# A macaron block on one core: layer-norm rows turned by DMA in float16 parts instead of by TensorE in float32

## The reference

```python
def _layernorm(x, axis=-1, eps=1e-05):
    m = jnp.mean(x, axis=axis, keepdims=True)
    v = jnp.var(x, axis=axis, keepdims=True)
    return (x - m) / jnp.sqrt(v + eps)

x = L0_attn_x                                   # (1, 4096, 256) float32
x = x + 0.5 * ffn(_layernorm(x))
x = x + attn(_layernorm(x))
x = x + 0.5 * ffn(_layernorm(x))

# ffn(x): six routed experts of rank 16, the two largest gates kept, beside a shared one
base_out = x @ base_W.T + base_b
shared_out = (x @ shared_A.T) @ shared_B.T
gate = softmax(x @ router_W.T + router_b)       # top 2, divided by their sum: sparse_w
routed_out = sum_e sparse_w[e] * (x @ routed_A[e].T) @ routed_B[e].T

# attn(x): 16 heads of 16, layer norm of q and k inside each head, causal
q, k, v = x @ Wq.T, x @ Wk.T, x @ Wv.T
dot = (norm(q) * s) @ (norm(k) * s).T           # s = 256 ** -0.25
out = softmax(causal(dot)) @ v
return out @ Wo.T + bo
```

## Time and profile before

| | |
|---|---|
| median of the runs | 1194.99 us |
| the three runs | 1192.07, 1194.99, 1195.09 us |
| span of the profiled execution, first to last instruction | 1192.3 us |
| PE busy | 1104.1 us (93% of the span) |
| ACT busy | 1014.7 us (85%), of it 982.2 us in the 1056 exponentials |
| DVE busy | 467.5 us (39%) |
| POOL busy | 241.6 us (20%) |
| chain of waits | 72% PE, 13% ACT, 6% issue, 6% DVE |

### The profile page before, as it was taken

One profiled execution on the slowest core, in us unless ns is written; L12 is line 12 of the kernel. 1 busy time (PEld: TensorE's weight loads), 2 busy tenths in 40 slices (PEclk: granted clock), 3 DMA queues, 4 the chain that ended last, 5 costly groups with the idle time before them and its releaser, 6 DMA issues.

```text
span 1192.3 us, 22761 instructions
## 1 busy us (share of the span) xinstructions
PE 1104.1 (93%) x8884; PEld 359.6 (30%) x8884; DVE 467.5 (39%) x1181; ACT 1014.7 (85%) x1134; POOL 241.6 (20%) x377
## 2 busy tenths in 40 slices
PE   3758999999999999999999999999999999999994
PEld 3534333332323233232332232232222222222123
DVE  5678665554544353333333323423131222021114
ACT  3216788789888998999999999999999999999980
POOL 2236533222122211212022021012110101010100
PEclk9779999999999999999999999999999999999996
DMA  5022202003000300003000022000001100000000
GB/s 145 3 63 60 59 11 81 1 28 99 1 1 19 93 17 1 1 32 92 4 1 1 1 67 60 1 1 2 1 10 48 53 1 1 10 10 1 1 19 18
DMA packets 39608, 33.37 MB, mean 28 GB/s; under 512 B 8722, under 2 KB 39432, under 8 KB 39496
## 3 DMA queue, kind: packets, MB, share of 16 engines
q1 hardware_dynamic: 37364, 31.74, 9.0%
q10 hardware_dynamic: 2132, 0.12, 0.1%
HBM read 18.73 MB, written 12.85 MB: 26 GB/s over the span
## 4 chain that ended last, share of the span: by engine, by line
PE 72%; ACT 13%; issue 6%; DVE 6%; DMA 1%; POOL 1%; SPq 0%; ACTq 0%; DVEq 0%; POOLq 0%
PE ps L1190 68%; ACT ring L776 13%; PE ps L1232 2%; PE ps L1298 1%; DMA x<-in_x 1%; DVE st L807 1%; PE ps L1252 1%; DVE area L828 1%; DVE oT L1159 0%; POOL rstd L711 0%; POOL sq L532 0%; DVE x L980 0%; DVE ss L985 0%; DVE sq L1013 0%; ACT area L765 0%
## 5 line engine op out<-in xcount | busy, mean ns | idle before, releaser
L776 ACT ACTIVATE ring<-ps 128x1024 f32<-128x1024 f32 x1056 | 982.2, 1115 | 65.5 <-PE ps L1190 63.5
L1190 PE MATMUL ps<-ring,vf 128*17 128x512 f32 (+3 forms) x4608 | 559.4, 562 | 5.0 <-DVE oT L1159 4.4
L1190 PE MATMUL ps<-queries,keys 50*128 50x512 f16 (+3 forms) x2304 | 363.2, 366 | 22.1 <-ACT ring L776 4.9
L1190 PEld LDWEIGHTS ps<-queries,keys 50*128 50x128 f16 x2304 | 92.3, 93 | 475.3 <-ACT ring L776 437.3
L724 POOL TENSOR_SCALAR_AFFINE_SELECT ring<-ring 128x256 f32<-128x256 f32 (+1 forms) x224 | 103.9, 481 | 396.5 <-ACT ring L776 392.6
L1190 PEld LDWEIGHTS ps<-ring,vf 128*17 128x17 f32 x4608 | 79.7, 95 | 174.5 <-issue 144.2
L711 POOL TENSOR_TENSOR rstd<-var,minus_half 128x4 f32<-128x4 f32 x24 | 24.4, 1017 | 235.6 <-DVE var L813 235.4
L980 DVE SCALAR_TENSOR_TENSOR x<-ps,power,x 128x512 f32<-128x512 f32 x32 | 24.0, 750 | 110.7 <-PE ps L1190 110.7
L846 DVE CAST xnT<-ps 128x512 f16<-128x512 f32 x32 | 22.1, 691 | 100.0 <-PE ps L1232 100.0
L1190 PE MATMUL ps<-baseT,xnT 128*128 128x256 f16 x384 | 55.0, 283 | 3.9 <-DVE area L848 3.8
L1232 PE MATMUL ps<-ident,area 128*128 128x128 f32 x192 | 34.2, 311 | 20.0 <-DVE area L828 20.0
(11 more groups left out here) (153 smaller groups left out, 670.5 us busy)
## 6 DMA issues: line engine op xcount, KB each, us to landing
parts_d<-split SPq DMA_DIRECT2D x32, 256.0 KB, 2.6
keys<-parts_d SPq DMA_DIRECT2D x96, 64.0 KB, 2.3
queries<-parts_d SPq DMA_DIRECT2D x192, 32.0 KB
x<-in_x SPq DMA_DIRECT2D x8, 512.0 KB, 4.2
out_x<-x SPq DMA_DIRECT2D x16, 256.0 KB, 2.2
queries<-shift_d SPq DMA_DIRECT2D x64, 4.0 KB
ring<-in_base_W SPq DMA_DIRECT2D x1, 256.0 KB, 4.9
ring<-in_Wq SPq DMA_DIRECT2D x1, 256.0 KB, 3.8
```

The costliest lines, as they stand in the source:

```text
L776: act.activation(probs[:, u % RING, :], bank(2 * (u % SLOTS), 2), ACTF.Exp, bias=0.0, scale=1.0).then_inc(exp_ok, 1)
L1190: return pe.matmul(o, lhsT, rhs, start=start, stop=stop, skip_group_check=True)
```

## The change

Layer-normed rows are no longer turned on TensorE. `turn{ln}` (c, a) is now: DVE casts two scaled tiles to float16 (the high part) and subtracts it (the low part), by tokens, in SBUF; then SP issues one DMA that transposes these 128 partitions x 1024 float16 numbers, eight blocks of 128x128, into `xnT`. The readers wait for that DMA's semaphore (`t_in`), not for a copy out of PSUM. `scale` of both halves now writes one small buffer, `xn`, so it alternates with `turn`. `xnT` and the parts of the attention's output are laid out by tiles. To make room, small buffers move into `ring` or are shared. Matrices, weights, the other transposes (`turnin`, `heads`) and the numbers in `PRELUDE` and `PLACES` stay.

```diff
-    for a in range(2):
+        # front() and prepare(): turn (c, a) now directly behind scale (c, a)
         yield 1.5, f"turn{ln}", (c, a)
...
-SPLIT_STAGES = ("turn0", "turn1", "turn2", "turnin0", "turnin1")
+SPLIT_STAGES = ("turnin0", "turnin1")
...
+            if stage in TURNS:
+                self.matmuls[stage, n] = through.get(int(stage[-1]))
             if stage in BANK_STAGES:
                 i = len(self.use)
+                through[turned_rows(stage, n)] = i + 1
...
+            def turn(K, stage, n):                       # on SP
+                (c, a), i = n, int(stage[-1])
+                sp.wait_ge(K.xs_ok[i], 2 * c + a + 1)
+                if K.matmuls[stage, n]:
+                    sp.wait_ge(K.ready, K.matmuls[stage, n])
+                if i == 2 and c == 0 and a == 0:
+                    sp.wait_ge(K.w_ok, NW)
+                sp.dma_start_transpose(xnT[i][:, 2 * a:2 * a + 2, :, :, :].rearrange("p n s b t -> p (n s b) t"),
+                                       xs[i][:, 2 * a:2 * a + 2, :, :].rearrange("p n s d -> p (n s d)")).then_inc(K.t_in[i][a], 16)
...
+            def split_rows(K, stage, n):                 # on DVE
+                (c, a), i = n, int(stage[-1])
+                high, src = moved(stage, n, None)
+                low = moved(stage, n, None, 1)[0]
+                if c >= 1:
+                    dve.wait_ge(K.t_in[i][a], 16 * c)
+                dve.wait_ge(K.xn_ok[i], 2 * c + a + 1)
+                dve.tensor_copy(high, src).then_inc(*K.own.up())
+                dve.wait_ge(*K.own.at())
+                dve.tensor_tensor(low, src, high, ALU.subtract).then_inc(K.xs_ok[i], 1)
...
-            def turn(K, ln, c, a):                       # on PE
-                key = (f"turn{ln}", (c, a))
-                b = side_bank(K, key)
-                pe.wait_ge(const, NCONST)
-                pe.wait_ge(K.xn_ok[ln], 2 * c + a + 1)
-                for ib in range(2):
-                    for i in range(2):
-                        m = pe.transpose(b[:, ib * D + i * P:ib * D + (i + 1) * P], xn[ln][:, 2 * a + i, ib * P:(ib + 1) * P], ident[:, :])
-                m.then_inc(K.ready, 1)
...
                 for a in range(2):                       # inner; project and value likewise
-                    pe.wait_ge(*K.done[f"turn{2 * f}", (c, a)])
+                    pe.wait_ge(K.t_in[2 * f][a], 16 * (c + 1))
```

More of the change, by code:

```diff
@@ L295, in general_order, with turned_rows @@
         yield stage, n
-BANK_STAGES = ("sizes", "turn0", "turn1", "turn2", "inner0", "inner1", "turnin0", "turnin1", "outer0", "outer1", "qk", "value", "heads",
+TURNS = ("turn0", "turn1", "turn2")
+BANK_STAGES = ("sizes", "inner0", "inner1", "turnin0", "turnin1", "outer0", "outer1", "qk", "value", "heads",
                "projout")
-SPLIT_STAGES = ("turn0", "turn1", "turn2", "turnin0", "turnin1")
+SPLIT_STAGES = ("turnin0", "turnin1")
+def turned_rows(stage, n):
+    if stage in ("inner0", "outer0"):
+        return 0
+    if stage in ("qk", "value"):
+        return 1
+    if stage == "projout":
+        return 1 if n[0] == NC - 1 else 2
+    return 2 if stage in ("inner1", "outer1") else None
 def on_scalar(stage, n):
-    if stage == "turn0":
-        return n[0] <= 3
     if stage == "turnin0":
         return n <= 3
-    if stage in ("turn1", "value"):
+    if stage == "value":
         return n[0] <= 2
-    if stage == "turn2":
-        return n[0] == NC - 1
     if stage == "turnin1":
@@ L348, in __init__ @@
         self.high_act = s("high_act")
+        self.xs_ok = [s(f"xs_ok{i}") for i in range(fronts + 1)]
+        self.t_in = [[s(f"t_in{i}_{a}") for a in range(2)] for i in range(fronts + 1)]
         self.xn_ok, self.var_ok, self.rstd_ok = ([s(f"{q}{i}") for i in range(fronts + 1)] for q in ("xn_ok", "var_ok", "rstd_ok"))
@@ L354, in __init__ @@
         self.parts_out = [s(f"parts_out{b}") for b in range(4)]
-        self.k_in = [[s(f"k_in{c}_{i}") for i in range(2)] for c in range(NC)]
+        self.k_in = [[s(f"k_in{c}_{i}") for i in range(2)] for c in range(2)]
         self.q_in = [s(f"q_in{g}") for g in range(NG)]
@@ L415, in build @@
         qn = area[1][:, :].rearrange("p (n c) -> p n c", n=TC)
-        xnT = [sb(f"xnT{i}", [P, 2, 2, CH], F16) for i in range(3)]
-        turners = xnT[2][:, :, :, :].rearrange("p s a t -> p (s a t)").bitcast(F32).rearrange("p (k c) -> p k c", c=P)
+        xnT = [sb(f"xnT{i}", [P, TC, 2, 2, P], F16) for i in range(3)]
+        turners = xnT[2][:, :, :, :, :].rearrange("p n s a t -> p (n s a t)").bitcast(F32).rearrange("p (k c) -> p k c", c=P)
         ones_sq = turners[:, NW, :]
@@ L557, in moved @@
         def moved(stage, n, b, part=0):
-            if stage in ("turn0", "turn1", "turn2"):
-                c, a = n
-                i = int(stage[-1])
-                return xnT[i][:, part, :, a * D:(a + 1) * D], bank(b).rearrange("p (b t) -> p b t", b=2)
+            if stage in TURNS:
+                a, i = n[1], int(stage[-1])
+                return xs[i][:, 2 * a:2 * a + 2, part, :], xn[:, :, :]
             if stage in ("turnin0", "turnin1"):
@@ L641, in _ @@
                     sp.dma_start(xg, x_v[:, c * TC:(c + 1) * TC, :]).then_inc(gen_in, 16)
-                    for b in BLOCKS:
-                        write_parts(gen, c, b)
+                    for stage, n in general_order(c):
+                        if stage in TURNS:
+                            turn(gen, stage, n)
+                        elif stage == "heads":
+                            write_parts(gen, *n)
                     for g in range(NG):
@@ L1090, in _ @@
             dve.wait_ge(*own.at())
[L1091 removed]
+            dve.tensor_reduce(bound[:, 4:8].unsqueeze(2), gain_rows, AX.X, ALU.add).then_inc(*own.up())
             dve.reciprocal(per, near).then_inc(*own.up())
@@ L1277, in project @@
                 for i in range(2):
-                    pe.wait_ge(*K.done["turn1", (c, i)])
+                    pe.wait_ge(K.t_in[1][i], 16 * (c + 1))
                 for ib in range(2):
-                    m = mm_parts(b, lambda s: xnT[1][:, s, ib, t], lambda s: qkT[:, s, ib, :], ib == 0, ib == 1)
+                    m = mm_parts(b, lambda s: xnT[1][:, k, s, ib, :], lambda s: qkT[:, s, ib, :], ib == 0, ib == 1)
                 m.then_inc(K.ready, 1)
@@ L1305, in front_and_heads @@
                     sizes(K, n)
-                elif stage == "turn0":
-                    turn(K, 0, *n)
-                elif stage == "turn1":
-                    turn(K, 1, *n)
                 elif stage == "inner0":
```

101 lines of the change are left out of this document (55 added, 46 removed).

## The result

| | before | after |
|---|---|---|
| median of the runs | 1195.04 us (1192.07 to 1196.54) | 1249.34 us (1249.03 to 1250.27) |
| span of the profiled execution | 1192.3 us | 1248.5 us |
| ratio | | 1.0461, interval 1.0443 to 1.048 |

A forecast was written before the change was run, and what follows sets the result against it. It took a chain over all engines as the bound to 120 us, TensorE from 120 to 700 us, ACT from 1000 us. 41.0 - 4 + 3.9 + 1.5 - 19.4 = +23 us gave 1218 us, range 1198 to 1245 us.

The forecast's parts named there:

- TensorE is the bound: 120 to 700 us: PE, busy 571.8 of 580 us, sets the time; exponentials wait a little for it.
- An operation taken from TensorE is worth its whole time: Removed float32 transposes, 120 to 1000 us: gain of 19.4 us, bounds 12 and 21 us.
- A to E: The start: five waits in a row on PE's queue, 41.0 us in sum (27.9 to 59.9).
- A: `inner0` of chunk 0: transposes stand behind SP's opening DMAs, 13.0 us late (10.1 to 17.5).
- B: `qk` 0: needs the third split in DVE's new order, 4.2 us late (1.3 to 7.9).
- D: `qk` 4: `fetch` (0, 0) stands between its two transposes on SP, 11.3 us late (8.6 to 15.1).
- E: `inner0` of chunk 2: split, issue, two fetches and landing make it 7.5 us late (4.8 to 11.3).
- Caught up, 4 us: After the start: DVE and POOL work ahead during PE's waits and PE had gaps, 4 us regained (3 to 6).
- mid-attention 1.5 us: Mid-attention: most DMA time is hidden; 1.5 us (0 to 4) for places late by a little.
- The end: Last `inner1`: two pairs of scales, two splits and the landing start it 3.9 us later (2.0 to 7.1).
- The blocks go one after another: Rival, chance 0.17: a DMA of eight blocks lands in 7.7 us or more; +46, 1241 us.
- SP the bound in mid-attention: Rival, chance 0.06: transposes wait behind keys or hold up fetches, some ten places; +12, 1230 us.

The follow-up runs named there:

- e5_quarter: Kernel before with three of the four transposes left out in 34 steady-part turns, no DMA in their place: 1194.22 us, ratio 0.9989.
- t1_outer: Kernel before without the six low-rank matmuls in each of 24 steady-part `outer`s: 1178.22 us, ratio 0.9861.
- s2_later: Changed kernel with SP's order of transposes and fetches changed around the first attention: 1243.79 us, ratio 1.0418.

## Why the prediction was wrong, step by step

**What bounds the kernel: failed, and it is the largest error.** "TensorE is the bound" from 120 to 700 us was read from 571.8 busy of 580 us. In fact PE's weight loads waited for exponentials for 204 of these 580 us, and TensorE needs 1.53 us for two units where ACT needs 1.84. The right view was the waits of the weight loads: 314.3 us for ACT from 300 to 1000 us, in the kernel before. The Trainium skill (Perfetto Trace Analysis, Identifying the Most-Contended Engine) calls matmul busy time a poor measure of how near a kernel is to its limit and takes the share of peak FLOPs and the weight loads' busy time instead. The trace agrees with the warning: matmuls were 93% busy, weight loads 30%, and `e5_quarter` took 16.6 us of the busy matmuls away for 1.3 us. Neither share says what a removed step is worth.

**"An operation taken from TensorE is worth its whole time": failed.** -19.4 us forecast, -0.2 us measured. The bound by which I took the smaller of PE's removed time and ACT's idle time is no estimate; ACT's idle time stood behind `outer`, `qk` and others, and none of it behind a `turn` (`t1_outer` -16.4 us, `e5_quarter` -1.3 us). The low end of 12 us for this term was no bound either: zero should have been in it.

**A to E: right in sum, 42.3 against 41.0 us**, by errors that cancel, which is luck. The landing was 3.1 us where I took 4.5, which alone would have made the five waits 7 us shorter; the issue 1.23 us as taken (1.2). A's high end of 17.5 us is above what its terms give (26.5 + 1.85 + 7.7 = 36.05 us, 16.9 us late). In A the first issue came at 31.23 us, not 26.5: SP finished the loads at 26.12 us and read its flag, and no row shows what it waited for after that. I had that read as free since SP had nothing to do behind it in the kernel before. In B the slow subtraction added 2.0 us. In D and E the order on SP was as read, and `s2_later` confirms it.

**"Caught up, 4 us" and mid-attention 1.5 us: failed with the other sign.** The kernel lost 10.7 us more between `inner0` 2 and 3. A typical case at 466 us stood for all; the tightest, `qk` 8, was the one to look up. It waited 7.1 us, `inner0` 3 another 1.6 us. The forecast also left out what a wait does to TensorE's clock. Behind the waits of `inner0` 2 and `qk` 8 it was granted at 0.50, the lower of its two levels (1.2 and 2.4 GHz; 141 to 146 us and 186.7 to 190 us), where the kernel before had 1.00. `inner0` 2 took 2.52 us there, before 1.42 us, and the first six matmuls of `qk` 8 took 2.72 us, before 1.47 us. From `inner0` 3 on the cover held: 0.4 us in one wait until the end.

**The end: right in sum**, 3.8 against 3.9 us. Of it 0.8 us came before the last `scale2`, which started at 1226.20 us, 53.6 us later than before, and 3.0 us behind it, with a landing of 3.1 us where 4.5 us was taken.

**Rivals.** "The blocks go one after another" forecast 1241 us, near the result for a wrong reason: the landing is 3.1 us for eight blocks. The Trainium skill (VectorE: DVE Perf Modes, The three transpose paths) gives 1309 ns for one block by DMA. Eight of them in a row would be 10.5 us, an estimate from that figure; in the trace eight in one DMA land in 3.1 us, so they don't add up so. The Trainium skill (DMA: Bandwidth & Descriptors, Latency and other measured facts) gives a transposing DMA 261 GB/s and any DMA a fixed cost of some 2 us. For 256 KB that makes about 3.0 us, an estimate; the trace agrees with 3.1 us. "SP the bound in mid-attention" didn't happen. A rival that the removed time is worth nothing stood nowhere.

## What to carry to other kernels

A matmul engine that shows 98% busy may still be waiting, as here: read what its weight loads wait for, and price a removed step by the waits of the other engine that stand right behind that step, not by its length. In this kernel a step that fits into the lead of one engine over the other was free, and the same microseconds in a longer step were not; a changed order changed which was which. A transfer put in place of an engine's work costs least where it has many microseconds of cover, and at a serial start it costs its issue, its landing and everything queued ahead of it.

## What the runs showed of the hardware

- In this kernel a transposing DMA from SBUF to SBUF, 128 rows of 1024 float16 values (eight 128x128 blocks, 256 KB), holds SP's queue for 1.23 us and lands 3.1 us after its issue (3.0 to 4.6).
- DVE's subtraction with both sources in SBUF took 0.69 us alone and 2.71 us beside GpSimd's addition of 128x1024 float32 values, 0.56 us beyond that addition's end; with the addition moved, 0.69 us. The Trainium skill (Trainium Architecture — The Big Picture, What this means for kernel authors) has a port pair that DVE and GpSimd share under an exclusive lock; the measurements fit it. Before, with a source in PSUM, it was 0.69 us.
- 64 columns less in 896 exponentials brought 23.3 us, and 136 more transposes of 0.163 us cost 15.0 us, on the same kernel: neither engine alone was the bound.
- After a wait of 7.14 us TensorE's granted clock was 0.50 from 141 to 146 us and 1.00 again from 147 to 158 us.
